# Two attention layers: projections, values and outputs from fp32 to three fp32r passes, routing from joined rows, scatters spread over steps

## The chip, the cores and the metric

One core of a Trainium2 chip runs the whole program as one launch. Engines: TensorE (PE; its weight loads are PEld), VectorE (DVE), ScalarE (ACT), GpSimd (POOL) and SyncE (SP), which issues most DMAs. The metric is the device time of one execution in microseconds, lower is better.

## The reference

`x` is 4 batches of 512 rows of 256 numbers. Two layers, each attention and a mixture of experts; every block's result is added to its input through a normalisation. Cut to what matters here:

```python
# layer 0: attention with 16 heads of 16, rotation, causal mask
xn = rms_norm(x, rms_w)
q, k, v = xn @ wq + bq, xn @ wk + bk, xn @ wv + bv      # 256x256 each
out = softmax(mask(rope(q) @ rope(k).T / 4)) @ v
y = out @ wo + bo + residual
# layer 0: experts, 8 of 256->1024->256, top 2, at most 640 rows each
probs = softmax(xr @ Wg); gate_vals, expert_idx = top_k(probs, 2)
dispatched = xr[dispatch_mask]; expert_out = relu(dispatched @ w1) @ w2
out = combine(gate_vals, expert_out)
# layer 1: attention (scale 1/16, no rotation), then gated experts of width 128, dense
```

The kernel computes in fp32 or in split products: a number is kept as an upper part in fp32r and a lower part (the remainder, also fp32r), and a product is three fp32r passes, upper by upper, upper by lower, lower by upper.

## The kernel before

The work runs in stages, each a block with a barrier at its end: `setup_phase` (clears buffers, loads rows and weights), `norm_phase` (statistics of batch 0), `attention_phase` for layer 0, `expert_phase`, `attention_phase` for layer 1, `dense_phase`.

**An attention phase** is a start and a loop. The start transposes batch 0 (`yt`), projects it (`pr`, four products of 128x512: queries and keys in two halves), computes the values (`v`), splits queries and keys into upper and lower parts, stores these pieces to DRAM and loads them back stacked by head (`load_stacks`). The loop has 16 steps T (a batch b and one of four groups g of four heads) and two more to drain; a step has 11 units s. In a unit TensorE does a part of the row maxima of step T (`max_unit`, fp32r; DVE reduces them with `unit_max`), a part of the probabilities of step T-1 (`prob_unit`; ACT takes the exponential), and what the plan `misc_plan` (L199) has put there. POOL masks the probabilities (`causal`), and in step T+2 TensorE multiplies them by the values (`pv`, fp32). Three banks hold maxima, two probabilities, one the values' product, two (`M_BANKS`) all else in turn.

**What the plan puts in.** `early` is started in unit 3 and evacuated in unit 5, `middle` in 6 and 8, `late` in 10 and unit 1 of the next step. For the batch after this one: transposes `yt`, projections `pr`, values `v`. For the batch before: `otr` (transposes the result of a step, DVE's `o_norm` divides by the row sums), `ot` (transposes of the whole batch), `out` (output product), then statistics, normalisation and joining to `x`. In layer 0 the routing follows: rows scaled by `route_rows`, `rt` (their transposes), `lg` (logits), `choose_top`, `choose_at`, `count`, `rk` (ranks) and `place`, then POOL's `scatter` writes each row twice to `dispatched`. Each engine runs its list in the order written in the loop over T and s, so an instruction that waits holds everything behind it on its engine.

**Lines that matter.** Projections, values and outputs are fp32 products (L938, L948), two TensorE matmuls each. ACT evacuates `yt` and `ot` (L662, L664, L699, L702) and frees the bank. In layer 0 POOL makes the residual with the output's bias (`residual`, L513 and L516), and DVE adds it (L1111). Joining is four scalings (`ln_normalise`, L1135) and one addition of 1024 columns (`ln_add`, L1141); `rt` waits for `route_rows` (L1153), which wait for POOL's root. In layer 0 the routing of batch 1 ends in steps 14 to 16, that of batch 2 in steps 16 and 17, with scatters in steps 14 and 17 and after the loop. w1 of the first expert is loaded in step 11, split by ACT in step 13 (2048 columns, L809) and by POOL in step 13 (L624). The first experts' rows are loaded after the barrier (L1652) and transposed (L1794). In layer 1 the start gathers the experts' rows (L562) up to eight tiles ahead and sums them (`combine_sum`, L1262 to L1268).

## Time and profile before

| | us |
|---|---|
| median of 3 runs (1113.88 to 1115.35) | 1114.74 |
| the profiled execution | 1114.21 |
| its span, first to last instruction | 1111.8 |

| engine | busy us | share of the span |
|---|---|---|
| PE | 943.1 | 85% |
| PEld | 760.3 | 68% |
| DVE | 611.4 | 55% |
| ACT | 473.8 | 43% |
| POOL | 455.5 | 41% |

The shares are means over stages of different kinds. Where the stages lie: the first maximum of the first attention starts at 40.9 us, its last step ends near 288, the first expert transpose is at 335.8, the second attention starts at 582.0, its loop at 625.0, and the last phase at 892.0.

### The profile page before, as it was taken

How to read it: one execution, taken by the hardware profiler on the slowest of the kernel's cores; microseconds unless marked ns; L12 is line 12 of the kernel's file. 1: busy time of each engine (PE TensorE's matmuls, PEld its weight loads, DVE VectorE, ACT ScalarE, POOL GpSimd, SP SyncE). 2: the span in 40 equal slices, each digit the busy share in tenths (PEclk: the TensorE clock that was granted, in tenths of full speed). 3: DMA queues.
4: the chain of work that ended last, by engine and by line, in shares of the span. 5: the costliest groups of instructions: out<-in, count | busy, mean ns of one | idle time of the engine just before them, and what ended most of it. 6: DMA issues, size and time to landing. Idle time of an engine off the chain costs nothing. (4 is left out here: it accounts for less than half of the span.)

```text
span 1111.8 us, 17858 instructions
## 1 busy us (share of the span) xinstructions
PE 943.1 (85%) x6122; PEld 760.3 (68%) x6122; DVE 611.4 (55%) x1970; ACT 473.8 (43%) x838; POOL 455.5 (41%) x429
## 2 busy tenths in 40 slices
PE   3799999868418999999982779899999779999996
PEld 1467767645318999999981446566667558888885
DVE  7577787956613343333435766776666334553534
ACT  2156555634103343333336245556556433343331
POOL 3354653555441333222336523445243534634232
PEclk9799999978757999999995889999999979999998
DMA  4443213210123323333103752532410010000001
GB/s 138 170 158 101 86 30 124 68 52 1 48 73 141 116 99 117 123 123 123 61 27 110 219 183 81 164 98 91 161 59 29 1 48 1 1 20 1 20 1 38
DMA packets 50312, 91.78 MB, mean 83 GB/s; under 512 B 7360, under 2 KB 23104, under 8 KB 50112
## 3 DMA queue, kind: packets, MB, share of 16 engines
q1 hardware_dynamic: 47168, 82.49, 22.3%
q0 software_dynamic: 3072, 8.39, 2.4%
q8 instruction: 38, 0.62, 0.2%
q14 instruction: 34, 0.28, 0.1%
HBM read 54.55 MB, written 36.31 MB: 82 GB/s over the span
## 5 line engine op out<-in xcount | busy, mean ns | idle before, releaser
L795 ACT ACTIVATE a_probs<-a_ps_b 128x512 f32<-128x512 f32 x320 | 187.4, 602 | 171.1 <-PE a_ps_b L859 168.7
L1063 DVE CUSTOM_DVE_ANT_0 a_masked_s<-a_ps_a,a_mask_f 128x512 f32<-128x512 f32 (+1 forms) x256 | 154.4, 621 | 116.0 <-PE a_ps_a L843 110.7
L843 PE MATMUL a_ps_a<-a_k_st,a_q_st 128*128 128x256 f32 (+3 forms) x512 | 191.3, 421 | 15.7 <-DMA a_k_st<-scratch 12.5
L494 POOL TENSOR_SCALAR_AFFINE_SELECT a_probs<-a_probs 128x512 f32<-128x512 f32 x128 | 79.6, 639 | 182.7 <-ACT a_probs L795 182.3
L1711 POOL TENSOR_TENSOR w_lo<-w_raw,w_hi 128x2048 fp32r<-128x2048 f32 x16 | 74.0, 4627 | 174.1 <-ACT w_hi L1728 174.1
L859 PE MATMUL a_ps_b<-a_q_less,a_k_st 128*128 128x384 f32 (+3 forms) x512 | 133.0, 323 | 6.6 <-ACT a_probs L795 5.5
L843 PEld LDWEIGHTS a_ps_a<-a_k_st,a_q_st 128*128 128x128 f32 x512 | 96.0, 199 | 55.7 <-issue 34.2
L859 PEld LDWEIGHTS a_ps_b<-a_q_less,a_k_st 128*128 128x128 f32 x512 | 89.2, 191 | 30.1 <-ACT a_probs L795 22.0
L883 PE MATMUL a_ps_pv<-a_probs,a_v 128*32 128x512 f32 (+3 forms) x1024 | 90.4, 476 | 8.8 <-POOL a_probs L494 8.8
L1926 POOL TENSOR_TENSOR dense_h_lo<-dense_mixed,dense_h_hi 128x512 fp32r<-128x512 f32 x40 | 52.2, 1306 | 102.5 <-ACT dense_h_hi L1983 102.5
L1776 DVE SCALAR_TENSOR_TENSOR exp_h_lo<-exp_ps_u,exp_h_hi 128x320 fp32r<-128x320 f32 x128 | 61.4, 490 | 59.0 <-ACT exp_h_hi L1737 58.2
L1822 PE MATMUL exp_ps_o<-w_hi,exp_h_hi 128*128 128x256 f32 x320 | 92.5, 289 | 0.0
L1737 ACT ACTIVATE exp_h_hi<-exp_ps_u 128x320 fp32r<-128x320 f32 x128 | 54.2, 438 | 89.6 <-PE exp_ps_u L1804 89.6
L1822 PE MATMUL exp_ps_o<-w_hi,exp_h_lo 128*128 128x256 f32 x320 | 90.4, 283 | 0.0
L1822 PE MATMUL exp_ps_o<-w_lo,exp_h_hi 128*128 128x256 f32 x320 | 90.4, 283 | 0.0
L1804 PE MATMUL exp_ps_u<-exp_x_t_hi,w_hi 128*128 128x320 f32 x256 | 80.4, 314 | 1.1 <-DVE exp_x_t_lo L1756 1.1
L1804 PE MATMUL exp_ps_u<-exp_x_t_lo,w_hi 128*128 128x320 f32 x256 | 80.2, 313 | 0.0
L1804 PE MATMUL exp_ps_u<-exp_x_t_hi,w_lo 128*128 128x320 f32 x256 | 80.2, 313 | 0.0
L883 PEld LDWEIGHTS a_ps_pv<-a_probs,a_v 128*32 128x32 f32 x1024 | 28.2, 116 | 66.7 <-issue 55.2
L2164 DVE TENSOR_TENSOR dense_product<-dense_gated,dense_ps_u 128x512 f32<-128x512 f32 x40 | 27.5, 687 | 78.5 <-PE dense_ps_u L2000 72.8
L1822 PEld LDWEIGHTS exp_ps_o<-w_lo,exp_h_hi 128*128 128x128 f32 x320 | 61.3, 191 | 0.0
L1822 PEld LDWEIGHTS exp_ps_o<-w_hi,exp_h_lo 128*128 128x128 f32 x320 | 61.3, 191 | 0.0
(267 smaller groups left out, 2217.6 us busy)
## 6 DMA issues: line engine op xcount, KB each, us to landing
w_raw<-in_m_w SPq DMA_DIRECT2D x16, 1024.0 KB, 5.7
scratch<-a_hi SPq DMA_DIRECT2D x24, 512.0 KB, 2.8
scratch<-a_lo SPq DMA_DIRECT2D x24, 256.0 KB, 3.4
a_q_st<-scratch SPq DMA_DIRECT2D x64, 96.0 KB, 2.6
a_k_st<-scratch SPq DMA_DIRECT2D x64, 96.0 KB, 2.6
exp_rows<-dispatched SPq DMA_DIRECT2D x9, 640.0 KB, 3.9
dispatched<-kept_sub SPq DMA_DIRECT2D x9, 512.0 KB, 2.9
results<-exp_out SPq DMA_DIRECT2D x7, 640.0 KB, 4.0
```

The costliest lines, as they stand in the source:

```text
L494: nc.gpsimd.affine_select(out=blocks, in_=blocks, compare_op=ALU.is_ge, fill=0.0, base=0, pattern=[[0, HPG], [1, P]], channel_multiplier=- ...
L795: nc.scalar.activation(probs[:, k, :], ps_b[k % B_BANKS][:, :], ACT.Exp, scale=scale).then_inc(exps, 1)
L843: last = nc.tensor.matmul(ps[:, at:at + wd], q_st[t % STACKS][:, h // PER_TILE, i * P:wd], k_st[t % STACKS][:, h, 0:wd], start=True, stop= ...
L859: last = nc.tensor.matmul(ps[:, at:at + wd], k_st[t % STACKS][:, h, j * P:(j + 1) * P], q_less[:, h // PER_TILE, j * P:SEQ], start=True, s ...
L883: last = nc.tensor.matmul(ps_pv[h * VW:(h + 1) * VW, at:SEQ], v[:, b % 2, j, g * HPG + h, :], rhs, start=(j == 0), stop=(j == 2), skip_gro ...
L1063: nc.vector.tensor_tensor_reduce(masked_s[n % 2][:, 0:wd], ps[:, 0:wd], mask_f[:, SEQ - wd:SEQ], -1.0, -NEG, ALU.add, ALU.min, nmax[:, t % ...
L1711: nc.gpsimd.tensor_tensor(of["lo"][:, :, :], of["raw"][:, :, :], of["hi"][:, :, :].bitcast(F32), ALU.subtract).then_inc(ready, 1)
L1737: nc.scalar.activation(h[0][:, f, half * HALF:(half + 1) * HALF], ps_u[n % U_BANKS][:, 0:HALF], ACT.Relu).then_inc(u_hi, 1)
L1776: nc.vector.scalar_tensor_tensor(h[1][:, f, cols], ps_u[n % U_BANKS][:, 0:HALF], 0.0, h[0][:, f, cols].bitcast(F32), ALU.max, ALU.subtract ...
L1804: last = nc.tensor.matmul(ps_u[(2 * f + half) % U_BANKS][:, 0:HALF], (w1["hi"], w1["lo"])[i][:, c, f * P:(f + 1) * P], x_t[j][:, c * CAP + ...
L1822: last = nc.tensor.matmul(bank[:, t % 2 * D:(t % 2 + 1) * D], h[i][:, f, t * P:(t + 1) * P], (w2["hi"], w2["lo"])[j][:, f, :], start=(f == ...
L1926: nc.gpsimd.tensor_tensor(h[1][:, (m - 1) % H_BUFS, :], mixed[(m - 1) % 2][:, :], h[0][:, (m - 1) % H_BUFS, :].bitcast(F32), ALU.subtract) ...
```

## The change

- Weights `qk`, `v`, `o` of both layers are loaded into the space of the probabilities, cast to upper parts by ACT (`weight_upper`), and DVE or POOL makes the remainder (`remainder`). ACT may write the first probabilities only when the remainders are done.
- `y_t` and `o_t` are pairs. ACT writes the upper part from PSUM; DVE writes the lower part from PSUM (`y_lower`, `o_lower`), one unit after ACT's evacuation, and frees the bank. Projections, values and outputs are three fp32r passes.
- Layer 0's output bias is one more pass of 64 rows in the output product; `residual` goes from POOL, and DVE's `out_evac` adds `x` times its factor to the product, one operation per tile.
- Joining is one operation per tile (`ln_join`, `combine_join`); the mean's part is left out of `x` and taken off in the last phase (`shift`).
- Logits come from the joined rows `x` with gate weights from which their mean is taken; the exponential takes the root as its scale. `rt` waits for joining alone. Routing of batch 1 is in steps 13 to 15, of batch 2 in steps 16 and 17. Placing has two operations fewer.
- Scatters: two tiles each in steps 14, 15, 16, then tiles 6 to 10, 11 and 12 to 15.
- w1 is loaded in step 9 and split in four pieces (ACT in steps 10 and 11, POOL in 11 and 12). SP waits for the scatters and loads the first expert's rows in the attention's block.
- The values' padding is packed from 32 to 17 columns a head, `mask_f` is bf16, gathered rows are four tiles deep.

```diff
+        if rope and b == BATCH - 2:
+            put(("ot", b, 0), T + 2, 2, T + 2, 4)
+            put(("ot", b, 1), T + 2, 3, T + 2, 5)
+            put(("out", b, 0), T + 2, 7, T + 2, 9)
+            put(("out", b, 1), T + 2, 9, T + 3, 0)
...
-        put(("rt", 1, 0), 13, 9, 13, 10)
-        put(("rt", 1, 1), 13, 10, 14, 0)
+        early(("rt", 1, 0), 13)
+        middle(("rt", 1, 1), 13)
+        late(("lg", 1, 0), 13)
         put(("rk", 0, 0), 14, 0, 14, 2)
-        middle(("lg", 1, 0), 15)
-        put(("rk", 1, 0), 16, 8, 16, 9)
-        put(("rt", 2, 0), 17, 6, 17, 8)
-        put(("rt", 2, 1), 17, 7, 17, 9)
-        put(("lg", 2, 0), 17, 9, 17, 10)
+        put(("rk", 1, 0), 15, 0, 15, 2)
+        put(("rt", 2, 0), 16, 0, 16, 2)
+        put(("rt", 2, 1), 16, 1, 16, 3)
+        put(("lg", 2, 0), 16, 3, 16, 5)
+        put(("rk", 2, 0), 17, 0, 17, 2)
...
+    LOWER_AT = {}
+    for (at_T, at_s), names in DONE_AT.items():
+        for name in names:
+            if name[0] in ("yt", "ot"):
+                LOWER_AT.setdefault((at_T, at_s + 1) if at_s + 1 < MAXES else (at_T + 1, 0), []).append(name)
...
             if rope:
                 sp.wait_ge(second_in, 16)
+                sp.wait_ge(scattered, 16 * 2 * TILES)
+                sp.dma_start(w1["rows"][:, :, :], w["dispatched"][0:CAP, :].rearrange("(p t) d -> p t d", t=CT))\
+                  .then_inc(keep["first_rows"], 16)
...
-                    if rope and T == 14 and s in (3, 5, 7, 9):
-                        scatter((s - 3) // 2)
-                    if rope and T == 17 and s in (3, 5, 7, 9):
-                        scatter(TPB + (s - 3) // 2)
+                    if rope and (T, s) in ((11, 3), (11, 4), (12, 3), (12, 5)):
+                        first_lower(2 * (T - 11) + s // (T - 7))
+                    if rope and T in (14, 15, 16) and s in (3, 8):
+                        scatter(2 * (T - 14) + s // 8)
...
             if rope:
+                for n in range(6, 11):
+                    scatter(n)
                 root(0, BATCH - 1)
+                scatter(11)
                 root(1, BATCH - 1)
-                for n in range(2 * TPB, TILES):
+                for n in range(12, TILES):
                     scatter(n)
...
                 elif kind == "pr":
-                    if half == 0:
-                        emptied(pe, ("yt", b, 0))
-                        emptied(pe, ("yt", b, 1))
-                    last = nc.tensor.matmul(ps[:, :], w_qk[:, half, n, :], y_t[:, half, :], start=(half == 0),
-                                            stop=(half == 1))
+                    pe.wait_ge(w_split["qk"], 1)
+                    pe.wait_ge(y_hi, b * KC + half + 1)
+                    for i, j in ROWS_LAST:
+                        if j == 1:
+                            pe.wait_ge(y_split, b * KC + half + 1)
+                        last = nc.tensor.matmul(ps[:, :], w_qk[i][:, half, n, :], y_t[j][:, half, :],
+                                                start=(half == 0 and i + j == 0), stop=(half == 1 and j == 1))
...
+                    if half == 0:
+                        pe.wait_ge(w_split[kind[0]], 1)
+                        pe.wait_ge(y_split if kind == "v" else o_split, (b + 1) * KC)
...
+            def y_lower(b, c):
+                name = ("yt", b, c)
+                dve.wait_ge(y_hi, b * KC + c + 1)
+                if rope:
+                    ins = nc.vector.scalar_tensor_tensor(y_t[1][:, c, :], bank(name)[:, :], rms_w[:, c:c + 1],
+                                                         y_t[0][:, c, :].bitcast(F32), ALU.mult, ALU.subtract)
...
+                ins.then_inc(free(name), 1)
+                emptied(dve, name)
+                dve.sem_inc(y_split, 1)
...
-                dve.wait_ge(resid_ready, n + 2)
-                nc.vector.tensor_tensor(sub[:, n:n + 2, :], bank(name)[:, :].rearrange("p (i d) -> p i d", i=2),
-                                        resid[:, 2 * half:2 * half + 2, :], ALU.add).then_inc(free(name), 1)
+                for i in range(2):
+                    last = nc.vector.scalar_tensor_tensor(tile(sub, n + i), tile(x, n + i), rstd[:, n + i:n + i + 1],
+                                                          bank(name)[:, i * D:(i + 1) * D], ALU.mult, ALU.add)
+                last.then_inc(free(name), 1)
...
+                nc.vector.scalar_tensor_tensor(tile(x, n), tile(sub, n), inv[:, i:i + 1], tile(x, n), ALU.mult,
+                                               ALU.add).then_inc(joined, 1)
```

## Rows read from the trace of the kernel before

In the tables of stretches (rows 1 and 2) the figures after the stretch are: its length, then PE, PEld, DVE, ACT and POOL busy, granted clock of PE (1.00 is 2.4 GHz), DMA share, GB/s. In the timelines: start us, us, engine, line, operation, out<-in, count, and in brackets the idle time before with its releaser.

**Rows 1.** by stage: stretch, us, busy us (x instructions) by engine, PEclk, DMA

```profile
40.90:207.90 167.00, 164.43 (x1102) 116.89 (x1102) 128.63 (x440) 92.13 (x166) 72.58 (x86) 0.98 0.33 108
207.90:265.40 57.50, 41.48 (x279) 28.89 (x279) 38.67 (x147) 24.82 (x43) 35.16 (x36) 0.85 0.11 33
265.40:335.80 70.40, 27.47 (x171) 19.04 (x171) 34.15 (x167) 11.17 (x22) 32.08 (x36) 0.68 0.16 55
...
582.00:625.00 43.00, 14.76 (x40) 8.42 (x40) 24.54 (x75) 23.95 (x37) 21.39 (x20) 0.65 0.39 128
625.00:867.00 242.00, 217.75 (x1406) 150.87 (x1406) 166.60 (x612) 130.83 (x238) 102.74 (x119) 0.95 0.37 115
```

**Rows 2.** same view: steps 5, 13, 14, 15 of the first attention

```profile
97.80:113.00 15.20, 15.20 (x94) 9.55 (x93) 10.76 (x33) 7.66 (x14) 9.67 (x12) 1.00 0.26 82
...
207.90:226.40 18.50, 10.55 (x78) 7.02 (x79) 17.01 (x58) 8.52 (x14) 11.85 (x10) 0.91 0.09 23
226.40:241.20 14.80, 14.71 (x95) 10.30 (x94) 10.06 (x45) 8.17 (x15) 6.47 (x7) 0.77 0.21 63
241.20:265.40 24.20, 16.21 (x110) 11.57 (x108) 11.61 (x45) 8.12 (x14) 16.84 (x19) 0.86 0.06 22
```

**Rows 3.** timeline, TensorE: fp32 weight load, fp32 products, then fp32r passes

```profile
28.04 0.19 PEld L938 LDWEIGHTS a_ps_m<-a_y_t,early_qk 128*128 128x128 f32 x1 [0.24 <-issue]
...
613.26 3.62 PE L948 MATMUL a_ps_m<-a_w_v,a_y_t 128*128 128x256 f32 x16
...
932.60 0.39 PE L2058 MATMUL dense_ps_x<-dense_mix_t,dense_select 128*128 128x512 f32 x1
932.83 0.28 PE L2000 MATMUL dense_ps_d<-dense_w_down_hi,dense_h_hi 128*128 128x256 f32 x1
932.95 0.28 PE L2000 MATMUL dense_ps_d<-dense_w_down_lo,dense_h_hi 128*128 128x256 f32 x1
```

**Rows 4.** timeline, steps 13 and 15 of the first attention: what waited

```profile
217.56 4.53 POOL L624 TENSOR_TENSOR w_lo<-w_raw,w_hi 128x2048 fp32r<-128x2048 f32 x1 [1.77 <-ACT w_hi L809]
...
217.82 4.90 DVE L1192 TENSOR_TENSOR a_hot<-a_numbers,a_top_atf 128x32 f32<-128x32 f32 x2
...
250.31 3.55 PE L883 MATMUL a_ps_pv<-a_probs,a_v 128*32 128x512 f32 x24 [6.29 <-POOL a_probs L494]
```

**Rows 5.** groups by line and form, whole run: mean ns, idle time before

```profile
L1069 DVE CUSTOM_DVE_ANT_0 a_masked_s<-a_ps_a,a_mask_f 128x256 f32<-128x256 f32 x128 | 48.8, 419 | 12.1 <-PE a_ps_a L843 10.6 <-DVE a_lo L1043 0.5 <-DVE a_prior L1197 0.3
...
L513 POOL TENSOR_SCALAR a_resid<-kept_x,kept_mean,kept_rstd 128x256 f32<-128x256 f32 x16 | 19.6, 1226 | 0.1
...
L1100 DVE TENSOR_TENSOR kept_sub<-a_ps_m,a_rsum 128x256 f32<-128x256 f32 x32 | 13.6, 424 | 1.1
...
L1265 DVE SCALAR_TENSOR_TENSOR kept_sub<-a_rows,gates 128x256 f32<-128x256 f32 x16 | 7.7, 484 | 0.6
...
L1023 DVE SCALAR_TENSOR_TENSOR a_part_q<-a_ps_m,early_bias,early_rot 128x512 f32<-128x512 f32 x8 | 6.0, 748 | 1.9 <-PE a_ps_m L938 1.9
...
L1141 DVE TENSOR_TENSOR kept_x<-kept_x,kept_sub 128x1024 f32<-128x1024 f32 x4 | 4.9, 1224 | 0.1
```

**Rows 6.** timeline from step 15 to the experts, and the page's DMA row

```profile
296.55 1.38 DVE L1135 TENSOR_SCALAR kept_sub<-kept_sub,a_moments,a_inv 128x256 f32<-128x256 f32 x4
...
304.19 1.94 PE L931 MATMUL a_ps_m<-kept_ident,kept_sub 128*128 128x128 f32 x8 [11.29 <-DVE kept_sub L1153]
...
310.49 0.19 DVE L1168 COPY a_logits<-a_ps_m 128x32 f32<-128x32 f32 x1 [6.44 <-PE a_ps_m L911]
...
325.24 0.97 POOL L554 DMA_INDIRECT dispatched<-kept_sub,a_put_at  x1 [0.30 <-issue]
...
335.81 0.48 PE L1794 MATMUL exp_ps_t<-kept_ident,exp_rows 128*128 128x128 f32 x1 [21.90 <-DMA exp_rows<-dispatched]
...
exp_rows<-dispatched SPq DMA_DIRECT2D x9, 640.0 KB, 3.9
```

**Rows 7.** timeline, setup: the clear of the padded values

```profile
5.61 1.76 DVE L1492 MEMSET a_v<- 128x2048 f32 x1 [0.38 <-issue]
```

428 lines of the change are left out of this document (255 added, 173 removed).

## The prediction

> **What bounds the kernel now.** I read the busy times by stage first, then by step of the attention loop, then the rows of single waits. By stage [rows 1]: in steps 0 to 12 of the first attention (40.9 to 207.9) TensorE is busy 164.4 of 167 us, so what leaves TensorE there shortens the time, unless a wait takes its place. Steps 13 to 15 are 57.5 us with TensorE busy 41.5. From the end of step 15 to the first expert (70.4 us) it is busy 27.5 us: a serial chain sets the time. The start of the second attention is 43 us with TensorE busy 14.8, again a chain; its loop is 242 us with 217.8 busy. Experts and the last phase keep their work and I leave them out but for one term.
>
> By step [rows 2]: step 5, a step with three projections and no routing, takes 15.2 us with TensorE never idle. Steps 13, 14 and 15 take 18.5, 14.8 and 24.2 us with TensorE busy 10.6, 14.7 and 16.2 us, at a mean granted clock of 0.91, 0.77 and 0.86, and they have no projections. So there are stalls in them, with their causes [rows 4]. In step 13 POOL's one lower part of w1 runs 4.53 us and the two small DVE comparisons beside it take 4.90 us. In step 15 TensorE waits 6.29 us for POOL's masking of the probabilities, which stood behind eight scatters and four pairs of residual operations.
>
> **The start of the first attention.** The clearing of the padded values (1.76 us on DVE [rows 7]) becomes two writes of a 64-column pattern. DVE ends the setup last, so I take 1.5 us. A bound is 0 (SP's issues end last) and 1.8. A weight tensor is now cast by ACT and its remainder made by DVE before the first projection. ACT is idle there, DVE needs 1.2 us (by the 1024-wide addition of rows 5), which fits while TensorE transposes and ACT evacuates, so I cost it at 0; uncovered it would be 1.2. The first batch's eight products of 512 columns begin at the lower level of the clock (1.2 GHz, half the granted clock), where an fp32 product costs 1.71 us (twice two of the 0.43 of rows 3) and three passes 1.40. Four of them lie on the way to the first stack: 1.2 us. The moved statistics let the keys be turned 0.7 us sooner: 1.9 in all. Sum of the start: 3.4 us (2 to 4.5) off the 40.9.
>
> **Three passes in the loops.** An fp32 product of 512 columns is two matmuls of 0.43 us (0.19 load plus 0.24 wait to the next load), 0.86; an fp32r pass has a pitch of 0.23 us (932.60 to 932.83), three are 0.70 [rows 3]. Saved: 0.155. For 256 columns: 16 matmuls in 3.62 us less the last one's tail are 0.215 each, 0.43 the product; three passes at a pitch of 0.12 are 0.36: saved 0.07. Steps 0 to 12 hold 24 products of projections (3.7 us), 24 of values (1.7) and 16 of outputs (1.1, less eight bias passes at 0.12, about 0.2 left): 5.6 us. Against that stands the new wait. The lower part is a DVE operation from PSUM of 0.75 us [rows 5], it frees the bank in place of ACT, and the next projection or output takes that very bank two units later. DVE then has the unit's maxima (two of 0.42, 0.77 together) and the normalisation (0.42 and a reciprocal, 0.67) of rows 5 ahead of it, 2.1 us against some 1.4 us of TensorE work: about 0.7 us of stall for each of three projections and two outputs, 3.5 us. Behind TensorE's wait queue the next maxima and probability units, and so ACT's exponentials. No row shows such a wait, so its bounds are 0 and 2.1 us each. Net 2.0 us (from 3 lost to 5.6 gained).
>
> **Steps 13 to 15.** What goes: the 4.53 us operation is in four pieces in steps 11 and 12 (POOL has over half of its time free there); the residual (16 operations of 1.23 us, rows 5, each with an addition behind it) leaves POOL for one DVE operation of 0.48 us per tile and the bias pass; eight scatters in step 14 become four in each of steps 14, 15 and 16. With this the 6.29 us wait has no cause. What is late next is DVE. Its own work in a step (maxima, split, one normalisation) is 8.5 us by step 5's busy 10.8 less three rotations of 0.75 [rows 2, 5] and somewhat less where it runs back to back; I take 8.0. Step 13 adds four row scalings and a choice and count of experts, some 5 us: 12.9. Step 14 now has a choice, count, placing, weighing, two lower parts and the first half of the output: 16.0. Step 15: second half, statistics, placing, weighing, joining: 15.9. TensorE would need about 12, 11.6 and 12 (step 5 less its projections, plus transposes). So I take DVE's pace: 44.8 us in place of 57.5, saved 12.7. The bounds are 5 (only the 6.3 us stall goes and DVE takes some back) and 21 (TensorE's pace).
>
> One rule bears on this. A DVE operation with two SBUF inputs stands still as long as POOL works from SBUF [rows 4]. The Trainium skill (SBUF — State Buffer, Who interferes with whom) says that a DVE instruction with two SBUF inputs contends with a GpSimd instruction that reads SBUF, and that one with at most one SBUF input outside the two-port modes doesn't. By that rule the trace agrees for the comparisons, the lower parts from PSUM are safe, and the new joins (two SBUF inputs) and DVE's remainders are not. From rows alone: a join can stand behind one POOL operation; taking half of the 1.23 us of rows 5 for each of step 15's four joins, that step is 2.5 us longer. I take 0 for it, since POOL has little left there, and count it to rival B.
>
> **From step 15 to the experts.** Steps 16 and 17 keep their exponentials and values; the third batch's transposes and logits move ahead of the last values, which frees about 1.1 us after them and adds 0.75 us of lower part; the masks come about 1 us sooner. The outputs are shorter. 2.4 us off (0 to 4). Then the chain [rows 6]. Before, the rows wait for POOL's root before TensorE may transpose (304.19), and the logits arrive at 310.49. After, TensorE transposes the joined rows: the scaling that begins at 296.55 (1.38 us) and the wide addition (1.22, rows 5) become four joins of 0.48, and the transposes start with the first of them, at about 297. The same transposes, copies and logits took 6.3 us (304.19 to 310.49); with 0.4 more for the last joins the logits are there at 303.7: 6.8 us. Placing loses two small steps: 0.4. The eight last scatters at 1.27 us (0.97 plus 0.30) still follow, since the others, six tiles, fit on POOL between the last mask and then. From the last scatter's start at 325.24 to the first expert transpose are 10.6 us, over a landing, the end of the block and a load of 3.9 us. After, SP issues the load as soon as the scatters land, beside the block's end: 3.4 us off. Sum 10.6 us (8 to 12.5).
>
> **The second attention.** At its start the chain has 0.9 us less for joining, and four products run at the lower clock before the second store, 0.31 us shorter each: 1.2 us. The remainders (2.6 us) lie in DVE's waits for gathered rows; the weight casts on ACT replace eight clears. 2.1 us off (0.5 to 3). In the loop 24 products of projections, 24 of values and 24 of outputs give 3.7 + 1.7 + 1.7 = 7.1 us, and six new waits at 0.6 take 3.6: 3.5 off. Here TensorE is idle a tenth of the time, so part of the gain may be lost in other waits: 0 to 7. The end gives 0.2, the shift in the last join costs two small DVE steps, 0.5. Sum 5.3 us.
>
> **The sum.** 3.4 + 2.0 + 12.7 + 2.4 + 10.6 + 5.3 = 36.4 us off the profiled execution's 1114.2 us (span 1111.8 and 2.4 around it): 1077.8. The median shown is 0.5 above that execution, so 1078.
>
> **Rivals.** A, the forecast: 1078, its own range 1069 to 1086. For it: both stalls have a named cause that is gone, and the tail is counted row by row.
> B, the lower parts and the joins make DVE the bound: the three-pass gain is eaten in both loops, and steps 13 to 15 give 7 rather than 12.7. For it: DVE is busy 128.6 of 167 and 38.7 of 57.5 us, and every lower part adds to it. Against: in steps 0 to 12 it still has over a fifth free. 3.4 + 0 + 7 + 2 + 10.6 + 1.5 = 24.5: 1090.
> C, DVE keeps ahead: no new wait, steps 13 to 15 near TensorE's pace. 3.4 + 5.6 + 20 + 2.4 + 10.6 + 7.5 = 49.5: 1065. Against: 16 us of DVE work in one step can't be hidden by 12 of TensorE.
> D, slower: the new waits for DVE leave TensorE idle in every fourth step and its granted clock falls from 2.4 to 1.2 GHz in the loops, as it does to a mean of 0.77 in step 14 after step 13's waits. Work at the lower level takes twice as long, so it decides from some 38 us of the two loops' 382 us of TensorE work at that level; with 60 us the time is 1137. Against: 0.7 us in a step of 13 is less idle time than the second attention's loop bears (a tenth of it) at a mean clock of 0.95 [rows 1].
> E, the passes don't run at the pitch of rows 3, so the precision change gives nothing: the three-pass terms (about 7 with the starts) go, 1085. Against: same forms and widths.
>
> **Chances.** A 0.55, B 0.25, C 0.12, D 0.04, E 0.04. The range reaches from just under C to just over B, 1063 to 1094; what lies outside is D and the tails of B and C, under 0.2. About 0.2% is what a measurement of this kernel can tell from no change: faster 0.95, same 0.01, slower 0.04.
>
> **What would show it.** Step 13 near 13, step 15 near 16 us with no TensorE wait for POOL's masks over 1 us; DVE the releaser of projections and outputs, some 0.7 us each (C: none; B: 2 us). First maximum near 37.5 us, logits-to-scatter chain as above, the first expert transpose about 7 us after the last scatter's start, some 31 us earlier in the span than 335.8. Experts and last phase unchanged within 1 us. The forecast is wrong if steps 14 to 16 take over 17 us each, if a wait for a weight's remainder shows in the starts, or if the clock in steps 0 to 12 is under 0.9.

## The result and the profile after

The changed kernel takes 1123.74 us (median of 4, 1120.7 to 1126.6) against 1115.05 (median of 4) of the kernel before on the same chip: ratio 1.0081, 95% interval 1.0061 to 1.0102. It is slower by 0.8%; 1078 had been forecast. One execution of one later kernel, the last with fp32 products, took 1556.18 us at a mean clock of 0.56 and is left out of that kernel's median. The profiled execution took 1126.60 us with a span of 1124.9 (before: 1111.8). On the page TensorE is busy 953.0 us (943.1 before) although each product was to become shorter, and DVE 621.2 (611.4). The span's 13.1 us split like this. A step ends where DVE's rounding of the row maxima (`a_nm`) starts; the changes were read at the same places in both traces.

| stretch | before | after | change | forecast |
|---|---|---|---|---|
| to the end of step 0 | 50.0 | 49.6 | -0.4 | -3.4 |
| steps 1 to 12 | 157.9 | 168.9 | +11.0 | -2.0 |
| steps 13 to 15 | 57.5 | 55.2 | -2.3 | -12.7 |
| step 15's end to the first expert | 70.4 | 68.2 | -2.2 | -13.0 |
| first expert to the end of step 0, second attention | 298.3 | 295.6 | -2.7 | -2.1 |
| its steps 1 to 15 | 232.9 | 239.5 | +6.6 | -3.5 |
| from there to the last phase's start | 25.0 | 26.9 | +1.9 | -0.2 |
| last phase | 219.9 | 221.0 | +1.1 | +0.5 |

The table of stretches for six steps of the first attention (1, 7, 11, 13, 14, 15; columns as in [rows 2]):

```profile
49.60:64.20 14.60, 13.73 (x66) 11.01 (x67) 10.60 (x33) 6.23 (x11) 4.26 (x5) 0.90 0.07 27
...
127.60:145.90 18.30, 18.30 (x132) 14.43 (x131) 11.34 (x42) 7.99 (x14) 6.63 (x7) 0.91 0.08 23
...
188.90:205.80 16.90, 16.90 (x132) 13.27 (x132) 11.63 (x42) 8.90 (x16) 4.72 (x6) 1.00 0.09 24
...
218.50:233.00 14.50, 13.74 (x103) 9.48 (x102) 11.40 (x57) 8.33 (x18) 2.98 (x5) 0.88 0.10 28
233.00:257.60 24.60, 18.89 (x107) 13.09 (x107) 14.78 (x72) 7.87 (x17) 5.46 (x6) 0.79 0.12 38
257.60:273.70 16.10, 12.73 (x93) 8.47 (x92) 14.97 (x61) 7.43 (x15) 8.77 (x11) 1.00 0.09 33
```

Step 7 was 15.5 us with TensorE at full clock before and is 18.3 with a mean clock of 0.91. Step 11, at clock 1.00 and TensorE never idle, has grown from 15.5 to 16.9: TensorE itself has more to do there (1.4 of it is the bias pass, below). Step 13 has lost its stall, as forecast (18.5 in [rows 2], 14.5 now; forecast 12.9), and step 15 too (24.2, now 16.1; forecast 15.9), but step 14 is 24.6 where 16.0 was forecast and 14.8 stood before. What TensorE waited for up to step 15 (engine, tile and line, releaser: us in total, times, longest; L1144 frees the bank of a lower part of `o_t`):

```profile
PE a_ps_m L1027 <- DVE a_y_t_lo L1123: 4.7, 3, 2.1
PE a_ps_m L1039 <- DVEq L1144: 4.7, 3, 2.1
```

The kernel before shows no such wait. Each of the six costs 1.2 to 2.1 us; five lie in steps 0, 4, 6, 8 and 10 and add up to 7.3 us, the sixth (2.1) in step 14. The one of step 6 in the timeline (DVE, then TensorE; a group of equal instructions is one row):

```profile
124.64 0.42 DVE L1187 CUSTOM_DVE_ANT_0 a_masked_s<-a_ps_a,a_mask_f 128x256 f32<-128x256 f32 x1
...
125.33 0.25 DVE L1216 RECIPROCAL a_rsum<-a_ps_m 128x16 f32<-128x16 f32 x1
125.62 0.42 DVE L1218 TENSOR_TENSOR kept_sub<-a_ps_m,a_rsum 128x256 f32<-128x256 f32 x1
125.96 0.74 DVE L1137 SCALAR_TENSOR_TENSOR a_o_t_lo<-a_ps_m,early_bias_v,a_o_t_hi 128x512 fp32r<-128x512 f32 x1
...
124.42 0.28 PE L921 MATMUL a_ps_a<-a_k_st,a_q_st 128*128 128x128 f32 x1
...
127.01 0.35 PE L1039 MATMUL a_ps_m<-a_bias_rows,a_spread_row 64*128 64x256 f32 x1 [1.39 <-DVEq L1144]
```

TensorE begins unit 10 at 124.42, when DVE is still in the maxima of unit 8; it begins those of unit 9 at 124.64 and then has the reciprocal, the scaling and the lower part before it, which ends at 126.70. TensorE is through with its own work of unit 10 at about 125.6 and waits to 127.01, 0.3 us past the lower part's end. Behind it, in stretches of 2 us (the column after POOL is the clock):

```profile
126.00:128.00 2.00, 0.99 (x5) 0.89 (x6) 1.77 (x5) 0.26 (x1) 1.22 (x2) 0.89 0.03 8
128.00:130.00 2.00, 2.00 (x8) 1.50 (x7) 0.70 (x2) 0.35 (x1) 0.00 (x0) 0.50 0.00 0
130.00:132.00 2.00, 2.00 (x13) 1.91 (x13) 0.30 (x1) 0.31 (x2) 0.00 (x0) 0.76 0.00 0
132.00:134.00 2.00, 2.00 (x21) 0.85 (x24) 1.79 (x6) 1.12 (x2) 1.40 (x2) 1.00 0.21 65
```

In finer stretches TensorE is granted 1.2 GHz from 127.5 to 131.0 us, from half a us behind the wait of 1.4 on, and 2.4 on either side; the same happens from 158.3 to 161.7 us, at the end of the wait of 2.1. In step 1 the clock, at its lower level since TensorE's wait for the first stacks (9.0 us, up to 39.49), rises near 52.4 us, where it rose near 48.8 before. In steps 1, 7, 8 and 9 the missing clock (length times one less the mean clock: 1.5, 1.6, 0.8, 1.0) adds up to an estimated 4.9 us.

The chain to the experts, from TensorE's, DVE's and POOL's timelines; it answers [rows 6]:

```profile
277.99 3.47 PE L961 MATMUL a_ps_pv<-a_probs,a_v 128*32 128x512 f32 x24
...
283.13 1.03 PE L990 MATMUL a_ps_m<-a_w_gc,a_ry_t 128*128 128x8 f32 x8 [1.25 <-ACT a_ry_t L774]
...
293.49 2.36 PE L961 MATMUL a_ps_pv<-a_probs,a_v 128*32 128x512 f32 x32 [0.80 <-POOL a_probs L554]
...
301.55 0.48 PE L1039 MATMUL a_ps_m<-a_bias_rows,a_spread_row 64*128 64x256 f32 x1 [2.29 <-DVEq L1144]
...
313.35 1.67 DVE L1255 SCALAR_TENSOR_TENSOR kept_x<-kept_sub,a_inv,kept_x 128x256 f32<-128x256 f32 x4 [1.16 <-POOL a_inv L571]
...
320.76 0.19 DVE L1283 COPY a_logits<-a_ps_m 128x32 f32<-128x32 f32 x1 [1.04 <-PE a_ps_m L990]
...
335.12 0.97 POOL L613 DMA_INDIRECT dispatched<-kept_sub,a_put_at  x1 [0.30 <-issue]
...
341.87 0.88 PE L1922 MATMUL exp_ps_t<-kept_ident,exp_rows 128*128 128x128 f32 x3 [17.68 <-DVEq L1878]
```

From the joining's start (313.35) the logits come 7.4 us later (before 296.55 to 310.49: 13.9), the last scatter starts 14.4 after them (14.8), the first expert transpose 6.7 behind that (10.6). These are 6.5, 0.4 and 3.8 us where the forecast had 6.8, 0.4 and 3.4: 10.7 in all against 10.6, with two terms off by 0.3 and 0.4 in opposite directions. But the joining starts 39.7 us after step 15's end, in place of 31.2. The last values (293.49) start 19.8 us after that end, where they started 13.2 after it (278.62), and the outputs (from 301.55) take 8.3 us in place of 5.4.

### The profile page after: what moved, and what is told of

It is laid out like the page before. It is cut to its first block and busy times, and to the rows that moved or that the text cites. A ratio compares the mean times of both kernels' runs of the same rounds, so it can differ in the third digit from the quotient of the medians.

```text
span 1124.9 us, 18414 instructions
## 1 busy us (share of the span) xinstructions
PE 953.0 (85%) x6334; PEld 787.7 (70%) x6334; DVE 621.2 (55%) x2023; ACT 478.8 (43%) x855; POOL 428.1 (38%) x404
## 5 line engine op out<-in xcount | busy, mean ns | idle before, releaser
L921 PE MATMUL a_ps_a<-a_k_st,a_q_st 128*128 128x256 f32 (+3 forms) x512 | 166.3, 373 | 16.8 <-DMA a_k_st<-scratch 14.2
L937 PE MATMUL a_ps_b<-a_q_less,a_k_st 128*128 128x384 f32 (+3 forms) x512 | 135.6, 329 | 4.5 <-ACT a_probs L871 3.6
L2055 POOL TENSOR_TENSOR dense_h_lo<-dense_mixed,dense_h_hi 128x512 fp32r<-128x512 f32 x40 | 52.4, 1310 | 102.9 <-ACT dense_h_hi L2112 102.9
```

The lines of the kernel that those rows point to most:

```text
L921: last = nc.tensor.matmul(ps[:, at:at + wd], q_st[t % STACKS][:, h // PER_TILE, i * P:wd], k_st[t % STACKS][:, h, 0:wd], start=True, stop= ...
L937: last = nc.tensor.matmul(ps[:, at:at + wd], k_st[t % STACKS][:, h, j * P:(j + 1) * P], q_less[:, h // PER_TILE, j * P:SEQ], start=True, s ...
```

## Experiments

Theory: TensorE waits for DVE's lower parts more than twice as long as I took, the clock falls behind some of these waits, the bias pass costs more than its pitch, and routing of batches 1 and 2 in steps 14 and 16 holds TensorE's list up. Rival: it is the rest of the change (routing, joining, scatters), not the three passes. Each kernel is the changed one with the edit shown. They ran on several chips, on which the kernel before took 1113 to 1122 us, so ratios to before are compared; 0.1% is 1.1 us.

**The bias pass.** TensorE's timeline in the changed kernel, one unit of step 11, and the same unit before:

```profile
194.82 0.40 PE L937 MATMUL a_ps_b<-a_q_less,a_k_st 128*128 128x512 f32 x1
195.15 0.38 PE L1039 MATMUL a_ps_m<-a_bias_rows,a_spread_row 64*128 64x256 f32 x1
195.46 0.39 PE L1044 MATMUL a_ps_m<-a_w_o_hi,a_o_t_hi 128*128 128x256 f32 x1
195.68 0.28 PE L1044 MATMUL a_ps_m<-a_w_o_lo,a_o_t_hi 128*128 128x256 f32 x1
...
196.44 0.40 PE L937 MATMUL a_ps_b<-a_q_less,a_k_st 128*128 128x512 f32 x1
```

```profile
184.38 0.40 PE L859 MATMUL a_ps_b<-a_q_less,a_k_st 128*128 128x512 f32 x1
184.62 1.03 PE L948 MATMUL a_ps_m<-early_o,a_o_t 128*128 128x256 f32 x4
185.29 0.53 PE L843 MATMUL a_ps_a<-a_k_st,a_q_st 128*128 128x384 f32 x1
185.66 0.39 PE L859 MATMUL a_ps_b<-a_q_less,a_k_st 128*128 128x512 f32 x1
```

From one probability product to the next the fp32 unit takes 1.28 us, the new one 1.62. The six passes have the pitch of 0.12 that [rows 3] gave. The bias pass, with 64 rows where all around it has 128, starts 0.09 us late, its successor comes 0.31 us behind it, and the next pass 0.22 behind that, where its neighbours have 0.12: some 0.5 us in all. Its weight load starts at 195.14, with its product and not ahead of it, and the next load at 195.45, again with its product, while the loads of its neighbours run a whole pass ahead (195.56 for the product at 195.68). The Trainium skill (TensorE: Matmul & The Clock Gate, Step-by-step: what each phase is for) says that a load is pulled ahead of a running product if the row groups don't conflict or it goes to the background buffer. By that rule nothing keeps back a load that goes to the background buffer; the trace doesn't agree for the load that follows the 64-row pass, and shows loads held on both sides of the change of shape. The experiment pads it with 64 rows of zeros:

```diff
-            bias_rows, spread_row = sb("bias_rows", [2 * VW, D], F32R), sb("spread_row", [P, P], F32R)
+            bias_rows, spread_row = sb("bias_rows", [P, D], F32R), sb("spread_row", [P, P], F32R)
...
-                        nc.tensor.matmul(ps[:, half * D:(half + 1) * D], spread_row[0:2 * VW, :], bias_rows[:, :], start=True,
+                        nc.tensor.matmul(ps[:, half * D:(half + 1) * D], spread_row[:, :], bias_rows[:, :], start=True,
                                          stop=False)
```

> The changed kernel with one edit: the output's bias pass in layer 0 has 128 rows (the 64 new ones are zero) in place of 64, so it has the shape of its neighbours. In the trace of the changed kernel a unit with two 256-column fp32r rows of passes and a bias pass takes 1.62 us (194.82 to 196.44), where the fp32 form took 1.28 us (184.38 to 185.66 before); the bias pass starts 0.09 us late, lasts 0.31 to the next start, and the pass behind it 0.22 where its neighbours have 0.12. Theory 1 (the change of shape costs it: the weight load is not hidden on either side): each of 16 bias passes falls to the pitch of 0.12, 0.38 us less, 12 in the loop and 4 in the tail: 4 to 6 us off the changed kernel's 1123.7, so 1118 to 1120, and a step with four output units falls from 16.9 to 15.5 us. Rival (the cost is an accumulation of a further pass, whatever its shape, or the time is set by the waits for DVE anyway): within 1 us of the changed kernel.

Measured: 1116.65, ratio 1.0031 (1.0015 to 1.0046), some 5.6 us less by the ratio. The same unit:

```profile
190.97 0.39 PE L939 MATMUL a_ps_b<-a_q_less,a_k_st 128*128 128x512 f32 x1
191.20 0.28 PE L1041 MATMUL a_ps_m<-a_bias_rows,a_spread_row 128*128 128x256 f32 x1
191.32 0.28 PE L1046 MATMUL a_ps_m<-a_w_o_hi,a_o_t_hi 128*128 128x256 f32 x1
...
192.20 0.39 PE L939 MATMUL a_ps_b<-a_q_less,a_k_st 128*128 128x512 f32 x1
```

1.23 us for the unit, 0.12 for the bias pass, its weight load at 190.98 ahead of the product at 191.20, and steps 7 and 11 are 15.5 us both. Theory 1 holds: doing twice the rows is 0.39 us cheaper. Of the 4.9 us by which steps 1 to 12 are shorter in this trace, 2.8 are the passes of steps 7 and 11 (1.4 each, by step 11); most of the rest lies in steps 1 and 7, where the clock was 1.00 this time, so a part of the 5.6 us is the clock.

**Where DVE makes the lower parts.**

```diff
                 for s in range(MAXES):
+                    for kind, lb, c in LOWER_AT.get((T, s), ()):
+                        (y_lower if kind == "yt" else o_lower)(lb, c)
                     if T < STEPS:
                         unit_max(T, s)
                     for name in DONE_AT.get((T, s), ()):
                         evac(name)
-                    for kind, lb, c in LOWER_AT.get((T, s), ()):
-                        (y_lower if kind == "yt" else o_lower)(lb, c)
```

> The changed kernel with one edit: in the loop's units DVE makes the lower parts of y_t and o_t ahead of that unit's maxima and evacuations instead of behind them. In the changed kernel TensorE waits in the first loop 1.4, 1.4, 1.2, 1.4, 2.1 and 1.2 us for a lower part or the bank that it frees, and 2.1 us in step 14, and its granted clock falls to 0.50 behind three of these waits (near 51, 128 and 160 us). Theory 1 (DVE's place in the queue is the cause, and the clock follows from the waits): most of 10 us of waits and some 4 us of lower clock in layer 0 go, and a smaller part in layer 1's loop (6.6 us longer than before): 8 to 15 us off 1123.7, so 1109 to 1116. Rival (DVE is short of time altogether: what is drawn ahead only makes the maxima late, and TensorE waits for a bank of maxima instead): within 3 us of 1123.7, with the wait moved to the maxima.

Measured: 1112.42, ratio 0.9982 (0.9969 to 0.9996): 11 us less. Steps 1 to 12 take 161.5 us in place of 168.9, at a mean clock of 1.00 in place of 0.97. The order of two entries in DVE's list decides whether the changed kernel is slower than the one before or level with it (0.2% faster).

**The three passes taken back.** `w_qk`, `w_v`, `w_o`, `y_t`, `o_t` are fp32 tiles without lower parts, and each three-pass loop is one product:

```diff
-                    for i, j in ROWS_LAST:
-                        if j == 1:
-                            pe.wait_ge(y_split, b * KC + half + 1)
-                        last = nc.tensor.matmul(ps[:, :], w_qk[i][:, half, n, :], y_t[j][:, half, :],
-                                                start=(half == 0 and i + j == 0), stop=(half == 1 and j == 1))
+                    last = nc.tensor.matmul(ps[:, :], w_qk[0][:, half, n, :], y_t[0][:, half, :], start=(half == 0),
+                                            stop=(half == 1))
```

> The changed kernel with the precision part undone: projections, values and outputs are fp32 products again (two matmuls each), no lower parts, no remainders; the bias pass, the joining, the routing, the scatters and the early load of rows stay as changed. It tells how much of the result is the three passes with their DVE work and how much is the rest. Theory 1 (the three passes with their waits cost what was to be gained): layer 0's steps 1 to 12 fall from 168.9 to some 159 us (before 157.9, plus 8 bias passes), layer 1's loop from 239.5 to some 233, the stretch of steps 13 to 15 from 55.2 to under 50, the time to 1098 to 1106. Rival (the rest of the change is what costs, by the routing that now shares steps 13 to 15): within 4 us of 1123.7.

Measured: 1105.71, ratio 0.9926 (0.9895 to 0.9958), 17 us less than the changed kernel. The rest of the change is a gain of 0.7%; the rival falls for the total. But step 14 is 23.8 us here too, so the passes are not what makes it long, and steps 13 to 15 take 54.5 us where theory 1 had under 50. Steps 7 and 11 are 17.5 us (15.5 before); with the padded bias pass, in the later run with fp32, they are 16.0.

**Step 14.** Its waits in the changed kernel (TensorE's, from 233.0 to 257.6):

```profile
PE a_ps_m L1039 <- DVEq L1144: 2.1, 1, 2.1
PE a_ps_m L950 <- DVE a_logits L1283: 1.3, 1, 1.3
PE a_ps_m L1039 <- DVE kept_sub L1229: 1.2, 1, 1.2
PE a_ps_m L1017 <- DVE a_picked L1320: 1.1, 1, 1.1
```

L950 waits for the logits' bank, L1017 for the ranks' bank, L1039 for a lower part of `o_t` and for the first half of the output. First, batch 1's choice, count, ranks and placing one step later:

```diff
-        put(("rk", 1, 0), 15, 0, 15, 2)
+        put(("rk", 1, 0), 16, 0, 16, 2)
...
-                    if rope and (T, s) in ((13, 4), (14, 4), (16, 6)):
+                    if rope and (T, s) in ((13, 4), (15, 4), (16, 6)):
...
-                    if rope and (T, s) in ((13, 8), (14, 8), (16, 7)):
+                    if rope and (T, s) in ((13, 8), (15, 8), (16, 7)):
```

> The changed kernel with the routing of batch 1 one step later: its choice and count on DVE move from step 14 to step 15, its ranks, placing and weighing from step 15 to step 16, the third batch's transposes and logits by one unit. Step 14 of the changed kernel is 24.6 us long; the trace shows TensorE waiting there 1.3 us for the bank of the logits, 1.1 us for the bank of the ranks, 2.1 us for a lower part of o_t and 1.2 us for the first output's bank, with the clock at 0.79 in the mean. Theory 1 (the waits in step 14 come from the place of outputs and lower parts, and the choice there only takes DVE time that is free): step 14 stays over 22 us, the time within 2 us of 1123.7. Rival (DVE's routing work in step 14 is what makes it late): step 14 falls under 18 us, step 15 grows by up to 2 us, and the time is 4 to 6 us lower.

Measured: 1125.95, ratio 1.0107 (1.0077 to 1.0137), step 14 at 22.8 us: DVE's choice isn't the main cause. Then the banks themselves:

```diff
-            put(("out", b, 1), T + 2, 9, T + 3, 0)
+            put(("out", b, 1), T + 2, 10, T + 3, 1)
...
-        put(("rk", 0, 0), 14, 0, 14, 2)
+        put(("rk", 0, 0), 14, 0, 14, 1)
...
                 for s in range(MAXES):
+                    for name in DONE_AT.get((T, s), ()):
+                        if name[0] in ("lg", "rk"):
+                            evac(name)
                     if T < STEPS:
                         unit_max(T, s)
```

> The changed kernel with one edit for step 14: DVE reads the logits and the ranks out of their banks ahead of the unit's maxima (the ranks one unit sooner), and the second half of batch 2's output product starts one unit later. Step 14 is 22.8 to 24.6 us long in the changed kernel and in all four kernels run so far, also with fp32 products (23.8) and with the choice of batch 1 moved away (22.8), so neither the lower parts nor the choice are its cause. Common to all are the waits of TensorE for banks of 1.3 us (logits), 1.1 us (ranks) and 1.2 to 1.6 us (first half of the output product), and a clock at 0.5 behind the first two, under which the 24 products of the values' unit take 2.9 to 3.6 us in place of 1.9. Theory 1 (these banks are the cause): step 14 falls to 17 to 20 us, the time by 5 to 8 us, to 1116 to 1119. Rival (DVE has more work in step 14 than fits, whatever the order; the waits only move): step 14 stays over 22 us and the time within 2 us of 1123.7.

Measured: 1122.75, ratio 1.0077 (1.0052 to 1.0102). Step 14 falls to 20.1 us, but step 15 rises from 16.1 to 18.7. Of its waits the ranks' is gone, the logits' bank costs 0.7, the output's 0.3, but the one for the lower part has grown to 2.5 us. Alone the edit is worth 2 us in the trace and nothing that the ratio can tell: neither expectation is met in full.

**Edits together.** Bias pass and lower parts first:

> The changed kernel with the edits of the first two runs together: the bias pass with 128 rows and the lower parts ahead of the unit's maxima. Alone they took 7.1 and 11.3 us off 1123.7 (to 1116.7 and 1112.4). In both, steps 7 and 11 fell to 15.5 us, in the one by the shorter output units and in the other because the clock stayed up, so a part is shared. Theory 1 (the places are different, the shared part is step 7's clock and the two output units' slack): 1105 to 1109. Rival (both only take away the same stretch of low clock, and the second gives nothing more): 1111 to 1113.

Measured: 1104.81, ratio 0.9922 (0.9895 to 0.9950); the two gains add. With step 14's banks as well:

> The changed kernel with all three edits (bias pass of 128 rows, lower parts first, step 14's banks). Theory 1 (three separate losses): 1097 to 1103, the first kernel of the change that is well under before's 1114.2. Rival (the serial chain behind step 15 takes back what step 14 gives, as POOL's scatters of batches 1 and 2 then end it): 1105 or more, with the stretch from step 15's end to the first expert transpose over 70 us.

Measured: 1102.10, ratio 0.9911 (0.9886 to 0.9937), step 14 at 17.4 us. And the same surroundings with fp32 products:

> As the run with all three edits, but with the projections, values and outputs as fp32 products (no lower parts, no remainders): what the three passes themselves are worth once their surroundings don't hold them up. Theory 1 (by the pitches, 0.155 us for a product of 512 columns and 0.07 for one of 256, less some waits that stay): it is 2 to 8 us slower than the run with three passes. Rival (the waits for DVE that are left eat it): it is within 1 us or faster.

Measured: 1097.73, ratio 0.9891 (0.9846 to 0.9937). With everything mended around them the three passes are at best level with fp32; the intervals overlap. Tables of stretches, steps 1 to 12 (and, for the first, 13 to 15): three passes, then fp32.

```profile
48.20:207.00 158.80, 153.28 (x1149) 115.76 (x1147) 127.19 (x431) 92.70 (x168) 63.47 (x75) 1.00 0.30 101
207.00:255.30 48.30, 39.67 (x298) 29.11 (x297) 40.85 (x188) 23.66 (x49) 17.15 (x22) 0.96 0.13 39
```

```profile
48.50:207.70 159.20, 156.85 (x1086) 112.14 (x1084) 123.50 (x421) 92.59 (x168) 63.33 (x75) 1.00 0.30 102
```

158.8 and 159.2 us. TensorE is busy 3.6 us less with the passes, and idle 3.2 us more. By step, those with three projections (5: 15.2 to 13.4) and with outputs and values (7: 16.0 to 14.1) gain 1.8 and 1.9 us; those in which lower parts are made (4, 6, 8, 10: 11.9, 11.6, 12.2, 11.8) lose 1.4, 1.6, 1.9 and 1.6.

**DVE's part priced alone.** In the kernel with three edits the loops make no lower parts and ACT frees the banks; TensorE's passes read the first batch's lower part of `y_t`:

```diff
-                    for kind, lb, c in LOWER_AT.get((T, s), ()):
-                        (y_lower if kind == "yt" else o_lower)(lb, c)
...
+                signal = y_hi if b == 0 else free(name)
-                    nc.scalar.mul(y_t[0][:, c, :], bank(name)[:, :], rms_w[:, c:c + 1]).then_inc(y_hi, 1)
+                    nc.scalar.mul(y_t[0][:, c, :], bank(name)[:, :], rms_w[:, c:c + 1]).then_inc(signal, 1)
```

> The kernel with the three edits, but in the loops DVE makes no lower parts of y_t and o_t (but for the last batch's o_t) and ACT frees the banks as in the kernel before; the passes with a lower part read the first batch's lower part of y_t instead, so TensorE does exactly the same work. Left out: batches 1 to 3's lower parts of y_t, batches 0 to 2's of o_t, so the result is less exact. It prices DVE's part of the three passes alone. The forecast had 12.7 us of saving by the passes' pitch in both loops against some 7 us of waits for DVE. In the traces the three-pass form with the lower parts first (against fp32 products with the same edits) gains 1.8 us in steps with three projections and 1.9 us in steps with outputs and values, and loses 1.3 to 1.9 us in each of the steps in which lower parts are made. Theory 1 (DVE's lower parts and the later freeing of the bank are all that is lost): the loops are 14 to 20 us shorter than with them, 1083 to 1088. Rival (the passes themselves hold the neighbouring units up, by their weight loads): 1096 to 1101.

Measured: 1086.88, ratio 0.9747 (0.9716 to 0.9777): 15 us under the kernel with lower parts by the medians (13 by the spans, 18 by the ratios) and 11 under fp32 (9 and 16).

```profile
48.80:202.80 154.00, 150.86 (x1148) 115.39 (x1146) 123.12 (x422) 92.70 (x168) 63.44 (x75) 1.00 0.31 104
202.80:247.80 45.00, 38.14 (x298) 27.65 (x297) 39.62 (x185) 23.49 (x49) 17.14 (x22) 1.00 0.14 42
```

The result is less exact, and TensorE runs the same passes as in the kernel with three edits; in steps 1 to 12 it is idle 3.1 us in place of 5.5, and its busy rows are 2.4 us shorter, which the trace does not explain. Steps 13 to 15 take 45.0 us. Against fp32 steps 1 to 12 are 5.2 us shorter, where the forecast had 5.6 for the passes alone: the pitches were right there, and DVE's side of it cost more than they save.

**Step 16.** The third batch's routing behind the last exponentials:

```diff
-        put(("rt", 2, 0), 16, 0, 16, 2)
-        put(("rt", 2, 1), 16, 1, 16, 3)
-        put(("lg", 2, 0), 16, 3, 16, 5)
-        put(("rk", 2, 0), 17, 0, 17, 2)
+        put(("rt", 2, 0), 17, 1, 17, 3)
+        put(("rt", 2, 1), 17, 2, 17, 4)
+        put(("lg", 2, 0), 17, 4, 17, 7)
-        final += [("rt", last, 0), ("rt", last, 1), ("lg", last, 0), ("rk", last, 0)]
+        final += [("rk", 2, 0), ("rt", last, 0), ("rt", last, 1), ("lg", last, 0), ("rk", last, 0)]
```

> The kernel with the three edits (1102.1, its profiled execution 1098.7) with one more: the third batch's routing is taken out of step 16. Its transposes come in units 1 and 2 of step 17 and its logits in 4 and 5, behind the last exponentials; its choice, count, ranks and placing lie beside the last output products and the last statistics; POOL writes its rows between the last roots. In the changed kernel the stretch from step 15's end to the last join's start is 39.7 us (31.2 before) although the chain behind the join is 10.7 us shorter as forecast: TensorE waits in step 16 for the transposed rows and the logits' inputs (1.2, 5.0 with the values at half clock, 1.3 us), the last values start 19.8 us after step 15 in place of 13.2, and the outputs take 8.2 us in place of 5.4. Theory 1 (the routing in step 16 holds up the last exponentials): the stretch to the join falls by 4 to 7 us, the time to 1095 to 1098. Rival (POOL's scatters of batch 2, now later, end last): the first expert transpose comes no sooner, within 1.5 us of 1102.1.

Measured: 1096.40, ratio 0.9840 (0.9809 to 0.9872), 0.7% under the kernel with three edits. Last values and joining in TensorE's and DVE's timelines (step 15 ends at 257.1):

```profile
269.75 1.93 PE L962 MATMUL a_ps_pv<-a_probs,a_v 128*32 128x512 f32 x24 [0.40 <-POOL a_probs L553]
...
289.81 1.67 DVE L1256 SCALAR_TENSOR_TENSOR kept_x<-kept_sub,a_inv,kept_x 128x256 f32<-128x256 f32 x4 [0.17 <-POOL a_inv L570]
```

12.7 and 32.7 us after step 15's end (19.8 and 39.7 in the changed kernel, 35.7 in the one with three edits). With fp32 products:

> The same with fp32 products for projections, values and outputs (the run with two edits and fp32, 1097.7, plus the later routing of batch 2). Theory 1: 4 to 7 us off 1097.7, 1091 to 1094, still some 3 us under the three-pass form. Rival (POOL's scatters end it): within 1.5 us of 1097.7.

Measured: 1095.29 (median of three, 1088.18 to 1097.04), ratio 0.9795 (0.9743 to 0.9848). By its ratio it is the fastest kernel here with the full computation, 2% under before, but level with the three-pass form within the intervals.

**The account closed.**

> The closing of the account: all four edits (128-row bias pass, step 14's banks, third batch's routing out of step 16, and no lower parts by DVE in the loops, where the passes read the first batch's lower part of y_t instead; left out are the lower parts of batches 1 to 3 of y_t and 0 to 2 of o_t). The four losses measured one by one are 7.1 (bias pass), 15.2 (lower parts where they are already first in the unit; 11.3 of the changed kernel's loss went by placing them first), 2.7 (banks) and 5.7 us (step 16). Theory 1 (these make up the difference between forecast and result): 1123.7 less 7.1, 11.8 (from 1116.7 to 1104.8 by placing first), 2.7, 15.2 and 5.7 is 1081; 1077 to 1084. Rival (the edits share the same stretches of low clock, or a further cause is missing): over 1086.

Measured: 1091.21 where before took 1121.79, ratio 0.9724 (0.9702 to 0.9746). On the forecast's scale (times 1114.7) that is 1084 (1081 to 1086), at the edge of theory 1's 1077 to 1084. On top of the lower parts' removal step 16's edit gave 0.2% (from 0.9747, the intervals overlap), where it had given 0.7 with them (0.9911 to 0.9840): the two may share something.

This does not close the account to 6 us. The forecast's 1078 had 7.1 us of waits for lower parts in it (3.5 and 3.6), and this kernel makes no lower parts in the loops, so by the forecast's own terms it should take 1071: some 13 us stay unassigned. (Leaving the lower parts out took 13 us off here by the ratios, 0.9840 to 0.9724, and 18 above.) Its trace, 4 us above its median, tells where to look. From step 15's end to the first expert it takes 63.5 us where 57.4 was forecast (61.2 in the kernel with three edits and step 16's). Its second loop takes 232.4 us (before 232.9), where the passes alone were to save 7.1.

**Another engine for the lower parts.** In layer 0's loop ACT reads the bank a second time into an fp32 tile and frees it, POOL subtracts in SBUF:

```diff
+            def pool_lower(name):
...
+                nc.gpsimd.tensor_tensor(t[1][:, c, :], whole[:, c, :], t[0][:, c, :].bitcast(F32),
+                                        ALU.subtract).then_inc(split, 1)
```

> The kernel with the three edits (1102.1), with DVE's lower parts in layer 0's loop given to ACT and POOL: ACT reads the bank twice (upper part in fp32r, whole value in fp32) and frees it, POOL subtracts in SBUF one unit later. In layer 1 DVE makes them, first in the unit, as before. Leaving all of DVE's lower parts out took 15.2 us off, some 7 of it in layer 0's loop (158.8 us from the end of step 0 to that of step 12 against 154.0). Theory 1 (what costs is that DVE is late; ACT with 8 of 13 us busy in a step and POOL with 5 have room): steps 1 to 12 take 154 to 157 us and the time is 1095 to 1099. Rival (the second read of ACT, 0.6 us, only moves the lateness: exponentials or POOL's masks behind it become late): steps 1 to 12 stay at 158 us or more, and the time within 2 us of 1102.1.

Measured: 1112.11, ratio 0.9919 (0.9894 to 0.9945), level with the kernel with three edits (0.9911). Steps 1 to 12 take 162.0 us: the rival's figures came, but not by the exponentials or masks that it named. Steps 4, 6, 8, 10 fell by 1.1, 1.1, 1.5 and 1.0 us, but the outputs waited (TensorE, 48 to 207 us):

```profile
PE a_ps_m L1065 <- POOL a_o_t_lo L562: 3.0, 2, 1.5
```

Steps 7 and 11 rose from 14.1 to 16.8 and 18.3 us. Together with step 16's edit:

> The same with the third batch's routing out of step 16 as well (that edit took 5.7 us off the kernel with three edits, to 1096.4). Theory 1: the two gains add, 1089 to 1094, the fastest kernel here with the full computation. Rival (POOL, which now has lower parts beside scatters in step 14, makes steps 13 to 15 longer by as much): 1095 to 1098.

Measured: 1110.78, ratio 0.9899 (0.9864 to 0.9933): theory 1 falls, and it is slower than the rival had it too. Then the transposes of the result two and three units sooner, with POOL's and with DVE's lower parts:

```diff
-            early(("ot", b, 0), T + 2)
-            middle(("ot", b, 1), T + 2)
+            at = 2 if rope else 3
+            put(("ot", b, 0), T + 2, at, T + 2, at + 2)
+            put(("ot", b, 1), T + 2, at + 1, T + 2, at + 3)
```

> The kernel with ACT and POOL making layer 0's lower parts and the third batch's routing out of step 16 (ratio 0.990 to before), with the transposes of the attention's result (ot) started in units 2 and 3 in place of 3 and 6 (layer 1: 3 and 4). In the run with POOL's lower parts the steps in which they are made fell from 13.3, 13.2, 14.1, 13.4 us to 12.2, 12.1, 12.6, 12.4, but the outputs then waited 1.5 us each for POOL's last lower part, and the clock fell behind it: steps 7 and 11 took 16.8 and 18.3 in place of 14.1 us. Theory 1 (only the time between transposes and outputs was too short): steps 7 and 11 return to 14.1 to 14.5, some 7 us less, ratio to before 0.982 to 0.985. Rival (ACT is the late one and stays late): ratio 0.987 or more.

> The kernel with DVE's lower parts first in the unit and the third batch's routing out of step 16 (ratio 0.984), with the same earlier ot. Theory 1 (DVE's lower parts cost by DVE's own load in the step, not by when the outputs need them): within 2 us, ratio 0.982 to 0.986. Rival (the waits before the outputs, 0.3 to 1.7 us each, are what is left): 4 to 6 us less, ratio 0.978 to 0.981.

Measured: 1108.31, ratio 0.9951 (0.9929 to 0.9973), and 1106.53, ratio 0.9938 (0.9922 to 0.9955). Both are slower than without the edit (0.9899, 0.9840), which only the first rival's open end (0.987 or more) allowed. Of the second, TensorE's waits from 48 to 265:

```profile
PE a_ps_m L952 <- DVE a_nm L1208: 5.8, 7, 2.7
...
PE a_ps_m L1019 <- DVE a_part_k L1115: 1.3, 2, 0.7
```

The waits in front of the product that takes the row maxima (L952) are 5.8 us where they were 3.1, and the transposes now wait for a bank that DVE's rotation frees (L1019). That fits two banks taken in turn, where a fill moved ahead meets the evacuation before it, but steps 1 to 12 are only 4.3 us longer, and the rest of the loss isn't traced. So what DVE's lower parts cost is not the wait in front of the outputs alone; how much is DVE's load and how much the later freeing of the banks no run here separates.

## Why the prediction was wrong, step by step

- **Start.** The forecast had 3.4 us. The first maximum starts at 39.5 us in place of 40.9 (37.5 forecast), and step 0 loses 1.0 of it to a 1.4 us wait for a lower part, the first of the new waits. The first transposes came 1.0 us sooner (15.57 for 16.59) where the clearing had been put at 1.5, and the projections ended 2.1 us sooner (27.42 for 29.49); what was lost from there to the first maximum no run here settles.
- **Steps 1 to 12, the passes.** Right: 5.6 forecast (for steps 0 to 12), 5.2 measured with the lower parts gone (154.0 against 159.2).
- **Steps 1 to 12, the new wait.** The mechanism was named, and its place, but "about 0.7 us of stall for each" is the term that failed. The five waits were 1.2 to 2.1 us, 7.3 in all where 3.5 had been forecast. The 2.1 us of DVE work was right (124.64 to 126.70 in the rows above). But TensorE's part was 1.2 us and not 1.4, DVE was 0.2 us late at the start of it, and 0.3 us pass from the lower part's end to TensorE's first pass: 1.4. In the wait of 2.1 us (158.44) DVE also had three statistics operations of the batch before (0.42 us each) among its maxima and began unit 8's only when TensorE was in unit 10. Nor did I carry the waits on: two brought the clock down for some 3.4 us each and the first kept it down, an estimated 4.9 us in all. The stated bounds were wrong too: five waits of 2.1 us against 5.6 of saving are 4.9 us lost, not 3.
- **The bias pass.** "Eight bias passes at 0.12" took the pitch of a 128-row pass for a 64-row one; no row of before had a change of shape inside a group, so it needed bounds and got none. It was some 0.5 us each, 16 of them (an estimated 6 us over the pitch; 5.6 us by the ratio, a part of which is the clock).
- **Steps 13 to 15.** Both named stalls went, and TensorE waits for no mask there. The 44.8 us came out at 45.0 (12.9, 15.7, 16.5) once the lower parts and the bank waits were gone, but that is partly luck: the sum counts two lower parts that this kernel doesn't make, and with step 16's edit the same steps took 48.2. Failed: step 14's 16.0 us, a sum of DVE's work. The 24.6 us come from the use of the two banks: logits, ranks, two transposes and two output halves in ten units, each freed by DVE behind a unit's maxima, with 5.7 us of waits at a mean clock of 0.79. The banks' edit took step 14 to 20.1 us, and to 17.4 with the other two edits (15.8 with fp32).
- **Step 15 to the experts.** The chain came as forecast (10.7 measured, 10.6 forecast, two terms off by 0.3 and 0.4). The 2.4 us ahead of it were wrong in sign. "Move ahead of the last values, which frees about 1.1 us" overlooked that step 16's transposes and logits stand ahead of the last exponentials in TensorE's list and wait there for ACT: the values came 6.6 us later, and the outputs, behind a wait of 2.3 us for a lower part that had been put at 0.75, took 2.9 us longer. Step 16's edit took the first back (12.7 us after step 15's end).
- **Second attention.** Start right (2.7 with the experts, 2.1 forecast). The loop lost 6.6 where 3.5 were to be gained. Without lower parts it took 228.4 us in one trace and 232.4 in another with the same instructions in this loop (before 232.9); the two differ in its first five steps alone. So the passes alone gave 4.5 or 0.6 us where 7.1 had been forecast: that term failed too, and its cause stays open.
- **Rivals.** B had the right mechanism, "the lower parts and the joins make DVE the bound", and priced it at a lost gain (1090), not at a loss. D's mechanism, the clock behind the new waits, came too, at an estimated 4.9 us in steps 1 to 12 and some 5 more than before in the second loop (mean clock 0.94, before 0.96), where I asked for 38 before it decided: together with B's and the bias pass it was enough. Giving each rival one mechanism, I had none in which two of them meet. E is out: the passes ran at 0.12 and 0.23 us.
- The Trainium skill's rule (SBUF — State Buffer, Who interferes with whom), whose price I kept out of the sum, was not what cost here: of the 16 joins one takes 0.96 us and the median is 0.48, what I had taken for them.
